# A routed expert layer on one core: which engine turns the gathered token rows

## The reference

```python
x = x + einsum('bsk,nk->bsn', layernorm(x), weight * block_mask)
h = layernorm(x)
logits = h @ W_gate + b_gate
_, top_idx = top_k(logits, 2)
y_all = relu(einsum('bsd,edh->bseh', h, W_e) + b_e)     # 8 experts, 1024 x 1024
y = mean over the two chosen experts of y_all
x = x + y
```

## Time and profile before

| | us |
|---|---|
| median of 3 runs | 670.69 |
| lowest and highest | 670.28, 671.13 |
| the profiled execution, its own time | 670.75 |
| its span in the profile | 669.0 |

### The profile page before, as it was taken

The page is one execution under the profiler, slowest core; times in us unless marked ns, Lnnn a source line. Parts: engine busy times, 40 slices in busy tenths (PEclk is TensorE's granted clock), DMA queues, the critical chain, the costliest instruction groups (busy, mean ns, idle before and its releaser), DMA issues.

```text
span 669.0 us, 10996 instructions
## 1 busy us (share of the span) xinstructions
PE 653.1 (98%) x3383; PEld 530.4 (79%) x3383; DVE 301.2 (45%) x563; ACT 353.3 (53%) x437; POOL 278.1 (42%) x255
## 2 busy tenths in 40 slices
PE   6999999999999999999999999999999999999994
PEld 5676777878878788888888888888888888888883
DVE  5886688877796554452451550433432440000000
ACT  7876854768675433545354535444543444465540
POOL 2013122225464365535544554455354545353431
PEclk9999999999999999999999999999999999999998
DMA  8991955698853489899698796689689885655210
GB/s 345 407 408 53 364 218 190 251 342 287 316 196 152 189 239 246 200 238 253 165 248 211 197 228 153 160 247 201 172 261 206 198 241 102 118 95 94 45 23 0
DMA packets 80884, 138.12 MB, mean 206 GB/s; under 512 B 49984, under 2 KB 49984, under 8 KB 80832
## 3 DMA queue, kind: packets, MB, share of 16 engines
q1 hardware_dynamic: 25776, 92.85, 38.2%
q0 software_dynamic: 11376, 33.57, 23.3%
q10 hardware_dynamic: 43680, 11.01, 9.8%
HBM read 87.59 MB, written 46.14 MB: 200 GB/s over the span
## 4 chain that ended last, share of the span: by engine, by line
PE 96%; DMA 1%; ACT 0%; SPq 0%; issue 0%; POOL 0%; DVE 0%; POOLq 0%
PE psO L509 86%; PE psT L799 2%; PE psT L509 2%; PE psT L542 2%; PE psO L542 1%; PE psG L615 1%; DMA xb<-data_t 1%; PE psS L596 1%; PE psT L583 0%; PE psT L627 0%; PE psT L604 0%; POOL rows_out L1796 0%; DVE w_stage L1426 0%; ACT xT L889 0%; ACT wT L903 0%
## 5 line engine op out<-in xcount | busy, mean ns | idle before, releaser
L509 PE MATMUL psO<-slots,xT 128*128 (+1 forms) x1872 | 430.2, 390 | 0.0
L509 PEld LDWEIGHTS psO<-slots,xT 128*128 128x128 f32 x1872 | 349.8, 188 | 71.9
L509 PE MATMUL psO<-wT,xT 128*128 128x512 f32 x624 | 152.3, 397 | 0.0
L1161 ACT ACTIVATE xb<-psO 128x512 f32<-128x512 f32 x78 | 46.6, 598 | 194.3 <-PE psO L509 189.0
L1414 DVE CAST slots<-raw 128x1024 fp32r<-128x1024 f32 x56 | 52.8, 942 | 187.1 <-PE psO L509 87.0
L509 PEld LDWEIGHTS psO<-wT,xT 128*128 128x128 f32 x624 | 114.3, 188 | 25.1 <-issue 2.7
L1784 POOL DMA_INDIRECT rows_out<-xb,tok_of x36 | 60.9, 1691 | 168.4 <-ACT xb L1161 159.9
L1778 POOL TENSOR_TENSOR xT<-x2T,xT 128x1024 fp32r<-128x1024 f32 x38 | 96.5, 2541 | 43.8 <-ACT xT L1123 30.2
L1416 DVE TENSOR_TENSOR slots<-raw,slots 128x1024 fp32r<-128x1024 f32 x56 | 72.8, 1300 | 1.9
L1074 ACT ACTIVATE psO<-bias_slot 128x512 f32 (+1 forms) x78 | 47.0, 602 | 38.1 <-ACT xb L1161 19.1
L1119 ACT ACTIVATE x2T<-turned 128x2048 uint16<-128x2048 uint16 x21 | 52.8, 2512 | 0.8 <-DMA turned<-x 0.8
(11 more groups left out here) (241 smaller groups left out, 542.4 us busy)
## 6 DMA issues: line engine op xcount, KB each, us to landing
raw<-L_ffn_W_e SPq DMA_DIRECT2D x56, 512.0 KB, 5.4
x_rows<-x SPq DMA_DIRECT2D x16, 512.0 KB, 4.6
xb<-data_t SPq DMA_DIRECT2D x12, 512.0 KB, 4.3
mask_stage<-mask_blocks SPq DMA_DIRECT2D x8, 512.0 KB, 10.7
w_stage<-weight_t SPq DMA_DIRECT2D x8, 512.0 KB, 11.4
row_stage<-L_attn_weight SPq DMA_DIRECT2D x8, 512.0 KB, 11.8
xr<-L_attn_data SPq DMA_DIRECT2D x8, 512.0 KB, 5.9
x_planes<-planes_even SPq DMA_DIRECT2D x8, 512.0 KB, 3.1
```

The lines of the kernel that those rows point to most:

```text
L509: last = eng.matmul(psum, xT[:, p, a, kt, :], moving(b, kt), start=(i == 0 and kt == 0 and not seeded), stop=(i == len(PASSES) - 1 and kt ...
L1161: eng.activation(xb[:, b % 2, n * HALF:(n + 1) * HALF], psO[:, n, :], ACT.Relu, scale=1.0 / TOP_K).then_inc(c_out, 1)
```

## The change

`TAIL` goes from 32 to 6, so every block from 5 on is turned by DMA, and TensorE turns blocks 0 to 4 alone. There are two buffers for turned rows instead of one: `turned_odd` where `turned` was, and `turned_even` over tables of the first part (`row_hot`, `gates`, `gated`, `ones`), which are laid side by side for that. The DMA transpose of every block is issued three blocks ahead, its gather four blocks ahead; even blocks from 6 on share one row buffer, odd ones another. The counter `l_turn` becomes a pair, one for each parity, and SP's table becomes two tables.

```diff
-    TAIL = 32
+    TAIL = 6
...
-        turned = at("turned", [P, 2 * KT, P], U16, xr_offset + D * 4)
+        turned = [at("turned_even", [P, 2 * KT, P], U16, routing_offset), at("turned_odd", [P, 2 * KT, P], U16, xr_offset + D * 4)]
...
         def gather_lead(b):
-            return 4 if by_dma(b) and not by_dma(b - 1) else 3
-
-        def turn_lead(b):
-            return 2 if by_dma(b - 1) else 3
+            return 4 if by_dma(b) else 3
...
+        def landed(b):
+            k = turns_of_dma(b)
+            return l_turn[k % 2], 16 * (1 + (k + 1) // 2)
...
                         if n == KT + 2:
-                            eng.wait_ge(c_pace, KT + 4)
-                        turned_by = after_turn[0:1, pair % (KT // 2), pair // (KT // 2) - 1:pair // (KT // 2)]
-                        eng.wait_ge(l_turn, eng.value_load(turned_by, min_val=16, max_val=16 * (N_TURNS + 1)))
+                            eng.wait_ge(c_pace, KT + 11)
+                        place_pair = (slice(0, 1), pair % (KT // 2), slice(pair // (KT // 2) - 1, pair // (KT // 2)))
+                        landed_by = [eng.value_load(after_turn[p][place_pair], min_val=16, max_val=16 * (turns_of_dma(LAST) + 1))
+                                     for p in range(2)]
+                        for p in range(2):
+                            eng.wait_ge(l_turn[p], landed_by[p])
...
+                elif k == 2:
+                    eng.wait_ge(c_ids, NB)
+                    eng.wait_ge(c_gate, NB)
+                    eng.wait_ge(c_logit, NB)
+                    eng.wait_ge(c_sums, NH)
+                    eng.wait_ge(c_unfold, 2)
                 else:
-                    eng.wait_ge(c_rhi, 2 * (b + 1 - turn_lead(b)))
-                eng.dma_start_transpose(turned[:], rows_of(b).bitcast(U16)).then_inc(l_turn, 16)
+                    eng.wait_ge(c_rhi, 2 * block_turned(k - 2))
+                eng.dma_start_transpose(turned_by(b), rows_of(b).bitcast(U16)).then_inc(l_turn[k % 2], 16)
...
-                    for c in (b + 2, b + 3):
-                        if n == 0 and c < N_BLOCKS and by_dma(c) and c - b == turn_lead(c):
-                            turn_rows(c)
+                    if n == 0 and b + 3 < N_BLOCKS and by_dma(b + 3):
+                        turn_rows(b + 3)
...
+                if b == TAIL - 5:
+                    eng.wait_ge(c_turn, SPARE_TURN)
+                    eng.memset(rows_of(TAIL), 0.0).then_inc(c_clear, 1)
                 for c in (b + 3, b + 4):
                     if c < N_BLOCKS and c - b == gather_lead(c):
                         gather_rows(c)
-                if b == TAIL - 4:
-                    eng.wait_ge(c_turn, turns_of_pe(TAIL - 6))
-                    eng.memset(rows_of(TAIL), 0.0).then_inc(c_clear, 1)
```

More of the change, by code:

```diff
@@ L115, in build @@
         row_sum = sb("row_sum", [P, NT], F32)
+        routing_offset = cursor[0]
+        row_hot = sb("row_hot", [P, N_EXP, P], F16)
+        gates = sb("gates", [P, KT, 32], F32)
         gated = sb("gated", [P, P], F32)
         ones = sb("ones", [P, P], F32)
+        assert cursor[0] == routing_offset + D * 4
         rows_b_offset = cursor[0]
@@ L327, in gather_lead, with turned_by, block_turned @@
         def gather_lead(b):
-            return 4 if by_dma(b) and not by_dma(b - 1) else 3
-        def turn_lead(b):
-            return 2 if by_dma(b - 1) else 3
-        SPARE_RING = turns_of_pe(TAIL - 6) % 3
+            return 4 if by_dma(b) else 3
+        SPARE_TURN = turns_of_pe(TAIL - 2) - 2
+        SPARE_RING = SPARE_TURN % 3
+        def turned_by(b):
+            return turned[turns_of_dma(b) % 2][:]
+        def landed(b):
+            k = turns_of_dma(b)
+            return l_turn[k % 2], 16 * (1 + (k + 1) // 2)
+        def block_turned(k):
+            return [b for b in range(N_BLOCKS) if by_dma(b)][k - 1]
         def ring_of(b):
@@ L498, in _ @@
             for p in range(2):
-                eng.wait_ge(l_add[p], 16 * added_by_end(p))
+                added = (N_BLOCKS - 1 - p) // 2 + 1
+                if p == LAST % 2:
+                    added += NH - 1
+                eng.wait_ge(l_add[p], 16 * added)
         @block.tensor
@@ L1148, in biases_of @@
                 return slot
-            eng.sem_inc(l_turn, 16)
+            for p in range(2):
+                eng.sem_inc(l_turn[p], 16)
             rows_hi(1)
@@ L1641, in _ @@
             eng.tensor_scalar(turn_part[:], turn_no[:], -3.0, None, ALU.add).then_inc(c_pace, 1)
-            eng.wait_ge(c_pace, KT + 1)
+            eng.tensor_scalar(tail_part[:], turn_no[:], float(5 - 2 * TAIL), 0.0, ALU.add, ALU.max).then_inc(c_pace, 1)
+            eng.wait_ge(c_pace, KT + 2)
             eng.tensor_scalar(turn_no[:], turn_part[:], 2, None, ALU.logical_shift_right).then_inc(c_pace, 1)
[L1644 to L1647, removed]
+            eng.tensor_scalar(tail_no[:], tail_part[:], 1, None, ALU.logical_shift_right).then_inc(c_pace, 1)
+            eng.wait_ge(c_pace, KT + 4)
+            eng.scalar_tensor_tensor(turn_part[:], turn_no[:], float(N_TURNS), tail_no[:], ALU.min, ALU.add).then_inc(c_pace, 1)
+            eng.wait_ge(c_pace, KT + 5)
+            eng.tensor_scalar(turn_no[:], turn_part[:], float(turns_of_dma(LAST)), 1.0, ALU.min, ALU.add).then_inc(c_pace, 1)
+            eng.wait_ge(c_pace, KT + 6)
+            eng.tensor_scalar(turn_part[:], turn_no[:], 1.0, None, ALU.add).then_inc(c_pace, 1)
+            eng.tensor_scalar(tail_no[:], turn_no[:], 1, None, ALU.logical_shift_right).then_inc(c_pace, 1)
+            eng.wait_ge(c_pace, KT + 8)
+            eng.tensor_scalar(tail_part[:], turn_part[:], 1, None, ALU.logical_shift_right).then_inc(c_pace, 1)
+            eng.tensor_scalar(after_turn[1][:], tail_no[:], 1.0, 16.0, ALU.add, ALU.mult).then_inc(c_pace, 1)
+            eng.wait_ge(c_pace, KT + 9)
+            eng.tensor_scalar(after_turn[0][:], tail_part[:], 16.0, None, ALU.mult).then_inc(c_pace, 1)
             for e in range(2, N_EXP):
@@ L1732, in gather_rows @@
                     else:
-                        eng.wait_ge(l_turn, 16 * (turns_of_dma(b - 2) + 1))
+                        eng.wait_ge(*landed(b - 2))
                     eng.indirect_dma_start(rows_of(b).bitcast(U16), None, x2_planes,
@@ L1827, in _ @@
                     add_last_rows()
-            for p in range(2):
-                eng.wait_ge(l_add[p], 16 * added_by_end(p))
 _INS = ["L0_attn_data", "L0_attn_weight", "L0_ffn_W_gate", "L0_ffn_b_gate", "L0_ffn_W_e", "L0_ffn_b_e"]
```

18 lines of the change are left out of this document (9 added, 9 removed).

## The result

| | kernel before | changed kernel |
|---|---|---|
| median of 7 runs, us | 670.80 | 717.87 |
| lowest and highest, us | 670.28, 671.13 | 683.76, 754.39 |
| the profiled execution, us | 670.75 | 754.39 |

The forecast was 659.0. Nearly as telling as the ratio is the spread: seven runs of one kernel lie up to 71 us apart, where those of before lie within 0.9.

The account below looks back on a forecast made before the run. TensorE's issue of matmuls and transposes was taken as the bound, busy 653.1 of 669.0 us. 670.75 less 11.7 for 13 gaps, all other terms nothing, gave 659.05, forecast 659.0 us; own range 658.2 to 660.2, with rival 1 658.2 to 664.0.

Parts of the forecast that it names:

- The saving on PE: On TensorE, 13 blocks no longer turned there save a gap of 0.90 us each, 11.7 us in all.
- ACT, DVE, SP as engines: Their added work costs nothing: ACT needs 7.9 of a block's 10.88 us, DVE has idle time, SP reads one more number.
- "10 or so" of 3 us each: Expected sign in SP's waits: 10 or so holds on turned rows in place of 5, 3 us each.
- that of POOL: Gathers wait for the transpose two blocks ahead, landing in 4.8, at worst 9.9 us; cost nothing, or at worst 1 us once.
- the ten blocks at the end: The last blocks, all DMA-turned, 10.88 us each without a gap, taken as evidence that transposes stay hidden.
- The weights' term: Weight loads and DVE's splits: stretch of 4 us taken, leaving 5 us for place 6 and 4 for place 1; no PE wait.
- two transposes that stop everything for their 4.8 us: Upper bound on the stretch of a place's weight stream: 9.6 us, a loss of 0.2 us for place 6.
- Rival 2: Late transposes hold up weight loads and starve PE: slower than before, 682 us at 7 us a transpose; chance 0.05.
- holds of 2.8 us: SP's average hold of weight loads for a transpose, cited against transposes stopping the loads altogether.
- Rival 3: ACT late with the joins, so PE waits 4.8 us for each DMA transpose: 51 us more, 721; chance 0.01.
- The engine price of a transpose by the row: On the DMA engines, one transpose takes 3.1 us of all 16, a weight chunk 1.4 us.
- Place 1: Its last split ends 7.9 us before PE wants it; 4 us left after the stretch, so no PE wait.

Follow-up runs that it names:

- e16: Changed kernel with all weight loads of places 1 to 7 but the first two cut to 32 of 1024 columns: 659.24 us, ratio 0.9823.
- e2: Changed kernel with the weight loads of places 2 to 7 cut to 32 of 1024 columns: 676.06 us.
- e4: Changed kernel with POOL making the low part ahead of the gather from block 6 on, so gathers start beside transposes: 733.98 us, ratio 1.0905.
- e10: The kernel of e4 with the weight loads of places 2 to 7 cut to 32 columns: 674.13 us.
- e11: Not identified in the text; either the changed kernel with four row buffers (683.52 us) or with gathers ahead of additions from block 10 on (770.14 us).
- e5: Changed kernel with ACT issuing a block's transpose only once the next block's gather has landed: 732.38 us.
- e9: The kernel of e1 with float32 gathers of PE-turned blocks from block 8 on issued beside a DMA transpose: 678.59 us, ratio 1.0099.
- e1: Changed kernel with TAIL back at 32, so even blocks up to 30 are turned by PE again: 669.67 us, ratio 0.9984.
- e3: Changed kernel with DMA transposes of even blocks from 8 on replaced by a copy of one of 16 column groups: 676.75 us, ratio 1.0124.
- e17: The kernel of e5 with the weight loads cut as in e16: 683.33 us.

## Why the prediction was wrong

**The saving on PE: right.** 13 x 0.90 us, and e16 gives 659.24 for the 659.0 on record.

**ACT, DVE, SP as engines: right in themselves.** In e16 ACT has 374.6 us of work, and of TensorE's waits in the expert blocks 0.4 us are left, all before 257 us. In the change itself SP's holds on turned rows came near what was told, 11 of them, 45.2 us in all, for "10 or so" of 3 us each.

**The step that failed is that of POOL** ("Nothing"), and with it the same assumption on ACT. Both took the landing of a transpose (4.8, at the worst 9.9 us) and of a gather from the trace before and moved them to a place where they run side by side under weight loads. Those numbers were measured where the two never meet under load: in the kernel before a gather of the planes goes out at 353.87 us and the next transpose at 364.47, and where they do overlap, in the last ten blocks, no weights are loaded. So my strongest evidence, the ten blocks at the end that "run in just this order without a wait", was evidence for two of the three transfers only. In the change, landings of 18 to 34 us took the place of 9.9, the worst that I allowed. POOL's gathers stood 166.8 us behind transposes, for a term put at nothing, and TensorE waited 61.5 us for the low part behind them. On ACT the issue of a transpose, taken as 5.7 us at the longest, took up to 9.7 (25.7 in e2), and behind it and the wait for the gather that goes ahead of it came the 13.7 us of TensorE's waits for the bias.

**The weights' term was sized with the right rows and asked the wrong question.** It asked whether the splits would be late for TensorE. DVE did wait longer for weights (198.1 us in the profiled run, 84.0 before), but no wait of TensorE is put down to a split; they are for the low part and the bias, which stand on POOL and ACT behind waits for gathers and transposes. A bound of "two transposes that stop everything for their 4.8 us" is no upper bound if a transpose can take seven times as long (34.2 us in e2).

**The rivals.** Rival 2 had the sign, and the reason in part (each transpose lands late under other traffic), and its example of 682 us lies by chance near the fastest run. But its place, the splits, was not where it struck, and 0.05 was too little. What I had against it, holds of 2.8 us, was again measured in the schedule that keeps gathers away. Rival 3 named what came, a transposition that is waited for, with a chance of 0.01 that was too low; but it came through the gathers and the low part, not through late joins. The engine price of a transpose by the row (3.1 us for 1.4 of a weight chunk) was the one sign that transposes are not ordinary traffic; I used it for volume alone.

**Place 1** was weighed for its splits and found safe (7.9 us). It was the first to crawl, in the profiles of the change and of e2, e4, e10 and e11, where the gather of block 6 now goes out within 1.0 us of the transpose of block 5 (0.2 in the change), and SP's holds do not cover the loads.

What is shown: the crawl comes with weight loads, a gather and a DMA transpose in flight together, and goes when the weights are taken away (e10, e16) or the gather is kept from the transpose (e5); gathers beside weights alone land in 8.8 us at most in the kernel before. In e9 the overlap costs 9 us with the old number of transposes, and in e1 the structure costs nothing. The number of transposes counts as far as it makes more such meetings (e3). Weight traffic costs time without a crawl too: 49 us lie between e17 and e5.

What stays open: why the DMA engines do this, and which of the parties they serve slowly. The additions of POOL were in flight in every kernel and were never taken away, so they may be a needed fourth; the same holds for the load of 512 KB of bias in each place. e16 has both and does not crawl, so they are not enough beside a gather and a transpose. And no kernel here keeps gather and transpose apart at no cost, so that the 659 us can be had with the weights is not shown.

## What to carry to other kernels

A latency read from a trace belongs to the company in which it was measured. Before a transfer is moved in time, list what else is in flight at its new place, kind by kind, and look for a stretch of the trace that has all of them at once; a stretch that has two of three proves nothing. And where a wait closes a loop over several engines, go round it once and add up all that stands in it, the instructions queued behind an issue too, and compare with the period: in e17 a gather of some 6 us stands in a loop of 11.7.

## What the runs showed of the hardware that I had not expected

- A gather of 0.5 MB, a DMA transpose of 0.5 MB and weight loads in flight together: 36 to 66 GB/s at a DMA share around 1 for some microseconds (e2), a transpose of 34.2 us (e2) and a gather of 33.8 (the change), against medians of 4.3 and 6.8 when kept apart under all weights (e5). Without weight loads the pair takes 6.2 and 6.4 (e10).
- Apart from gathers, the transposes were faster with all weights loaded (e5: 4.3 us at the median, at most 8.1) than in the kernel before (5.9 and 9.9).
- The issue of a DMA transpose holds ACT's queue, and the relu behind it, for 1.3 to 9.7 us in the change, and for 25.66 us once in e2.
- The Trainium skill (DMA: Bandwidth & Descriptors, Rules for kernel authors) says, of what is to be serialised, that a transpose next to ordinary DMAs needs nothing. No run here speaks against that for the data. For the time the traces do not agree where a gather is among these DMAs: transposes land in 11.9 us at the median and 32.6 at most in e4, where the gathers start beside them, and in 4.3 and 8.1 in e5, where they are kept away; and e9, with the overlap, is 9 us slower than e1 without it.
- The mean granted clock fell to 0.948 in the longest run of the change, and stood at 0.50 in the longer waits of TensorE and just behind them, so that a wait of DMA origin cost matmul time as well: 8.4 us more busy time with 11.7 us less work.
